# Attention with a running memory: the product with the probabilities made as columns, memory's part added after the transposes

## The reference, cut to what matters

```
sigma_q = elu(q) + 1;  sigma_k = elu(k) + 1
att_dot = softmax(mask(q k^T / scale)) @ v
att_mem = sigma_q @ mem / (sigma_q @ z)
delta   = v - sigma_k @ mem / (sigma_k @ z)
mem    += sigma_k^T @ delta;   z += sum(sigma_k)
att     = beta * att_mem + (1 - beta) * att_dot
out     = att.reshape(B, 64, 16*128) @ Wo
```

## Time and profile before

| | us |
|---|---|
| median of 3 runs | 1669.26 (1668.77 to 1669.92) |
| the profiled execution | 1669.3 |
| its span, first to last instruction | 1667.5 |
| PE busy | 1623.2 (97%) |
| DVE busy | 1143.7 (69%) |
| ACT busy | 884.9 (53%) |
| POOL busy | 497.9 (30%) |

### The profile page before, as it was taken

The page is one execution under the profiler, slowest core; times in us unless marked ns, Lnnn a source line. Parts: engine busy times, 40 slices in busy tenths (PEclk is TensorE's granted clock), DMA queues, the critical chain, the costliest instruction groups (busy, mean ns, idle before and its releaser), DMA issues.

```text
span 1667.5 us, 42642 instructions
## 1 busy us (share of the span) xinstructions
PE 1623.2 (97%) x17190; PEld 1418.9 (85%) x17190; DVE 1143.7 (69%) x3508; ACT 884.9 (53%) x1955; POOL 497.9 (30%) x438
## 2 busy tenths in 40 slices
PE   6899999999999999999999999999999999997998
PEld 5798999899998989998999989998999989875555
DVE  6865858586775757575776758585867757688544
ACT  5664646465563646364654646464655636451131
POOL 2332323232332313231333323232323323130351
PEclk9999999999999999999999999999999999998999
DMA  5102121212202121212112021212011021228847
GB/s 183 49 21 77 35 78 33 79 30 58 58 29 85 34 71 33 86 33 68 38 44 74 29 77 36 77 33 79 31 57 58 29 88 34 73 97 263 266 90 215
DMA packets 121780, 122.06 MB, mean 73 GB/s; under 512 B 24032, under 2 KB 101296, under 8 KB 121456
## 3 DMA queue, kind: packets, MB, share of 16 engines
q1 hardware_dynamic: 118224, 113.52, 22.3%
q0 software_dynamic: 3328, 5.81, 1.8%
q10 hardware_dynamic: 32, 0.01, 0.0%
HBM read 94.90 MB, written 24.40 MB: 72 GB/s over the span
## 4 chain that ended last, share of the span: by engine, by line
PE 93%; DVE 5%; issue 1%; ACT 1%; DMA 0%; DVEq 0%; ACTq 0%
PE bank_p L1473 23%; PE bank_v L1591 13%; PE chain_k L1546 6%; PE chain_k L1524 6%; PE bank_a L1481 5%; PE bank_v L1481 5%; PE chain_q L1524 5%; PE bank_s L1494 4%; PE chain L1524 3%; PE bank_a L1562 3%; PE bank_p L1504 3%; PE bank_p L1648 2%; PE bank_v L1573 2%; PE bank_a L1573 2%; PE bank_s L1579 2%; PE chain L1546 2%
## 5 line engine op out<-in xcount | busy, mean ns | idle before, releaser
L588 POOL TENSOR_TENSOR step_place<-step_place 128x512 f32<-128x512 f32 x128 | 166.7, 1303 | 575.5 <-ACT step_place L734 426.5
L756 ACT ACTIVATE step_place<-chain_q,step_place 128x128 f32<-128x128 f32 x384 | 113.3, 368 | 225.3 <-DVE step_place L990 225.3
L1591 PE MATMUL bank_v<-step_place 128*128 128x256 f32 x1024 | 225.3, 381 | 0.7 <-ACT step_place L767 0.7
L1473 PE MATMUL bank_p<-xt_hi,w_hi 128*128 128x256 f32 x1024 | 220.0, 296 | 4.6 <-DVE w_lo L911 2.5
L1591 PEld LDWEIGHTS bank_v<-step_place 128*128 128x128 f32 x1024 | 193.2, 190 | 29.2 <-issue 2.6
L1473 PE MATMUL bank_p<-xt_hi,w_lo 128*128 128x256 f32 x1024 | 206.6, 283 | 0.0
L1473 PE MATMUL bank_p<-xt_lo,w_hi 128*128 128x256 f32 x1024 | 206.4, 283 | 0.0
L625 POOL TENSOR_TENSOR step_place<-step_place 128x512 f32<-128x512 f32 x64 | 69.4, 1084 | 433.2 <-DVE step_place L1251 433.2
L1473 PEld LDWEIGHTS bank_p<-xt_hi,w_hi 128*128 128x128 f32 x1024 | 158.4, 191 | 24.0 <-issue 14.5
L978 DVE SCALAR_TENSOR_TENSOR step_place<-step_place,bank_p 128x512 f32<-128x512 f32 x128 | 87.5, 684 | 109.3 <-ACT bank_p L728 109.2
L1473 PEld LDWEIGHTS bank_p<-xt_hi,w_lo 128*128 128x128 f32 x1024 | 160.0, 192 | 0.0
(11 more groups left out here) (219 smaller groups left out, 3959.8 us busy)
## 6 DMA issues: line engine op xcount, KB each, us to landing
step_place<-in_L_attn_Wo_dram SPq DMA_DIRECT2D x128, 256.0 KB, 2.7
step_place<-beta_all SPq DMA_DIRECT2D x64, 256.0 KB, 3.4
expert_place<-in_L_ffn_w_dram SPq DMA_DIRECT2D x24, 512.0 KB, 7.6
expert_sums<-zero SPq DMA_DIRECT2D x16, 272.0 KB, 4.9
expert_rows<-rows_place SPq DMA_DIRECT2D x15, 288.0 KB, 2.3
step_place<-in_L_attn_x_dram SPq DMA_DIRECT2D x16, 256.0 KB, 3.9
turned<-in_L_attn_x_dram SPq DMA_DIRECT2D x16, 256.0 KB, 3.9
x_rows<-rows_place SPq DMA_DIRECT2D x16, 256.0 KB, 2.8
```

The lines of the kernel that those rows point to most:

```text
L588: nc.gpsimd.tensor_tensor(dl[seg][:, :, 0:DK], val[:, seg, :, :], beta_rows[:, :, :], ALU.mult).then_inc(s["vb_ready"], 1)
L756: ins = nc.scalar.activation(to[:, j, :], t[:, at:at + DK], ACT.Copy, scale=rd[:, seg, r:r + 1])
L1473: ins = mm(out, w[:, g, m, c, col], x[:, c, :, :].rearrange("p s t -> p (s t)"), start=i == 0, stop=i == len(parts) - 1)
L1591: ins = mm(bank_v[:, b * D:(b + 1) * D], att[:, b * PIECES + i, :], wo[:, i % WR, :], start=(i == 0 and b == 0), stop=(i == PIECES - 1), s ...
```

## The change

The product is made the other way round: `vo` (64 partitions x 128 columns) is the stationary operand and `pt` (64 x 64) the moving one, so that the result has the 128 value dimensions as rows and the queries as columns. It fills all 128 columns of the array and half its rows, as the matmuls of `update` do. Sequence 0 goes to `bank_a`, sequence 1 to `bank_v`. This result is already turned, so ACT copies it into `att` (now before `read_out` at the head of its step, each copy writing with a step of 128 elements between neighbours). The memory's read `am` alone goes through the transposes, and DVE adds the turned banks onto `att`; these additions now stand behind the first `sigma_k` of the step. One `by_piece` matrix suffices, since both segments of `am` now lie alike; the other is gone, with two instructions of GpSimd at the start.

```diff
@@ ScalarE: attended
-            for seg in range(2):
-                act.wait_ge(s["att_mm"], 2 * n + seg + 1)
-                rows = att[:, :, :].rearrange("p a (s g m) -> p a s g m", s=2, m=HG * QR)
+            act.wait_ge(s["av_mm"], n + 1)
+            for b in range(B):
+                rows = att[:, b * PIECES:(b + 1) * PIECES, :].rearrange(
+                    "p a (s g m) -> p s g m a", s=2, m=HG * QR)
                 nc.scalar.activation(
-                    rows[:, :, seg, g, :], seg_bank[seg][:, :].rearrange("p (a m) -> p a m", m=HG * QR),
-                    ACT.Copy).then_inc(s["att_ready"], 1)
+                    rows[:, :, g, :, :],
+                    seg_bank[b][:, :].rearrange("p (s m a) -> p s m a", s=2, m=HG * QR),
+                    ACT.Copy).then_inc(s["av_kept"], 1)
@@ ScalarE: body
+                if n:
+                    attended(n - 1, (g - 1) % NG, None if first or g == 0 else blk)
                 read_out(n, 0)
...
-                if n:
-                    attended(n - 1, (g - 1) % NG, None if first or g == 0 else blk)
@@ VectorE: attended
-            dve.wait_ge(s["av_mm"], n + 1)
             for seg in range(2):
-                dve.wait_ge(s["am_ready"], 2 * n + seg + 1)
-                t = (am[0][:, n % 2] if seg == 0 else am[1][:, 0]).rearrange("p j d -> p (j d)")
-                nc.vector.tensor_tensor(t, t, seg_bank[seg][:, :], ALU.add
-                                        ).then_inc(s["att_summed"], 1)
+                dve.wait_ge(s["att_mm"], 2 * n + seg + 1)
+                t = att[:, :, :].rearrange("p a (s g m) -> p a s g m", s=2, m=HG * QR
+                                           )[:, :, seg, n % NG, :]
+                nc.vector.tensor_tensor(
+                    t, t, seg_bank[seg][:, :].rearrange("p (a m) -> p a m", m=HG * QR), ALU.add
+                    ).then_inc(s["att_ready"], 1)
@@ VectorE: body
-                if n:
-                    attended(n - 1)
                 dve.wait_ge(s["s_mm"], n + 1)
...
                     sigma_k(n + 1, 0)
+                if n:
+                    attended(n - 1)
@@ TensorE: numerators
-                    half = b if seg == 0 or kind == 0 else 1 - b
-                    ins = mm(t[ROWS[half], at:at + ZC], sig[:, j, seg, b, :],
+                    ins = mm(t[ROWS[b], at:at + ZC], sig[:, j, seg, b, :],
@@ TensorE: attend
-                        half = b if seg == 0 else 1 - b
-                        ins = mm(seg_bank[seg][ROWS[half], j * DK:(j + 1) * DK],
-                                 pt[ROWS[b], j, seg, :], vo[ROWS[b], seg, j, :],
-                                 start=True, stop=True)
+                        c = (seg * HG + j) * SEG
+                        ins = mm(seg_bank[b][:, c:c + SEG], vo[ROWS[b], seg, j, :],
+                                 pt[ROWS[b], j, seg, :], start=True, stop=True)
@@ TensorE: attended_transposes
+            pe.wait_ge(s["av_kept"], 2 * n + 2)
             for seg in range(2):
-                pe.wait_ge(s["att_summed"], 2 * n + seg + 1)
+                pe.wait_ge(s["am_ready"], 2 * n + seg + 1)
...
-                    ins = nc.tensor.transpose(out[:, :, :, j, :], t[:, j, :], by_piece[seg][:, :])
+                    ins = nc.tensor.transpose(out[:, :, :, j, :], t[:, j, :], by_piece[:, :])
```

More of the change, by code:

```diff
@@ L43 @@
 KSCALE = 1.0 / (DK ** 0.5)
-STEP_PLACE = 24545
+STEP_PLACE = 24417
 def stand_alone(eng, noted):
@@ L205, in layer @@
     ident = sb("ident", [128, 128])
-    by_piece = [take([128, 128]) for i in range(2)]
+    by_piece = take([128, 128])
     turned = sb("turned", [128, NC * B * BLK])
@@ L274, in layer @@
              "s_masked s_max s_shifted s_exp s_inv p_ready pt_ready "
-             "rdk_ready rdq_ready mem3_ready wo_used x_turned dl_ready am_ready mem_ready att_summed att_ready "
+             "rdk_ready rdq_ready mem3_ready wo_used x_turned dl_ready am_ready mem_ready av_kept att_ready "
              "x1_ready x1_normed x1_stored x1t_mm x1t_ready x1t_stored lg_mm lg_exp "
@@ L555, in _ @@
         nc.gpsimd.memset(ident[:, :], 0.0).then_inc(s["ident_ready"], 1)
-        for i in range(2):
-            nc.gpsimd.memset(by_piece[i][:, :], 0.0).then_inc(s["ident_ready"], 1)
-        pool.wait_ge(s["ident_ready"], 3)
+        nc.gpsimd.memset(by_piece[:, :], 0.0).then_inc(s["ident_ready"], 1)
+        pool.wait_ge(s["ident_ready"], 2)
         nc.gpsimd.affine_select(out=ident[:, :], in_=ident[:, :], compare_op=ALU.not_equal,
@@ L561, in _ @@
                                 ).then_inc(s["ident_ready"], 1)
-        for i in range(2):
-            nc.gpsimd.affine_select(out=by_piece[i][:, :], in_=by_piece[i][:, :],
-                                    compare_op=ALU.not_equal, fill=1.0, base=-SEG * i,
-                                    pattern=[[-SEG + 2 * SEG * i, 2], [-1, PIECES], [-PIECES, QR]],
-                                    channel_multiplier=1).then_inc(s["ident_ready"], 1)
+        nc.gpsimd.affine_select(out=by_piece[:, :], in_=by_piece[:, :],
+                                compare_op=ALU.not_equal, fill=1.0, base=0,
+                                pattern=[[-SEG, 2], [-1, PIECES], [-PIECES, QR]],
+                                channel_multiplier=1).then_inc(s["ident_ready"], 1)
         nc.gpsimd.memset(mask[:, :], 0.0).then_inc(s["const_ready"], 1)
@@ L1616, in pick_transposes @@
                                 ident[:, :]).then_inc(s["pickt_mm"], 1)
-        pe.wait_ge(s["ident_ready"], 6)
+        pe.wait_ge(s["ident_ready"], 4)
         pe.wait_ge(s["x_normed"], 1)
```

## The result

The changed kernel takes 1747.72 us (median of 4 runs, 1746.33 to 1748.64) against 1669.01 of the kernel before, a ratio of 1.0471 with a 95% interval of 1.0455 to 1.0486: 79 us slower. The prediction said 1750 in a range of 1710 to 1768. Two of its executions, the traced one among them, took 1748.6 us at a mean granted clock of 0.989, the other two 1746.3 and 1746.9 at 0.993 and 0.992.

What follows compares the result with a forecast made beforehand. PE was taken to bound the kernel, busy for 97% of the span. 1669.3 us + 47 for PE's product + 34 for waits behind DVE's additions = 1750 us, range 1710 to 1768.

Steps and rivals of the forecast that it cites:

- PE's product: From `update` to `scores`: 16 matmuls with 128 stationary columns, 0.110 us apart, 0.74 us more a step, 47 us in all.
- The overflow of DVE: DVE's additions before `state_last` exceed its idle time, so PE's second half of the queries waits: 2.15 us a block, 34 in all.
- ACT hidden: ACT's two copies at the head of the step, some 0.6 us each, fit its 3.05 us idle before `read_out`: no cost.
- The bound, 1.5 us a copy: At the head of the step, ACT's copies cost time only beyond about 1.5 us for one copy.
- The rival built on DVE's accesses: Stepped access doubles DVE's additions to 1.19 us each: some 72 us on top, 1822 us; chance 0.06.
- PE waiting at the transposes for ACT: Sign that the prediction is wrong: ACT's copies should end before `read_out` is ready; no size given.
- the hidden overflow: Rival: loads set PE's pace in the product, but DVE's additions cause no visible wait: 1717 us; chance 0.18.
- the pace of the moving columns: Rival: moving columns set the product's distance at 0.062 us, with DVE's overflow still paid: 1701 us; chance 0.08.
- the upper bound: Top of the range, 1768 us: distance 0.113, additions 0.04 us longer, wait 0.15 us longer in each of 45 steps.

## Why the prediction was right

- PE's product: said 0.74 us a step from a distance of 0.110 us, measured 1.93 - 1.24 = 0.69, at 0.112. The small difference is mostly in the first distances behind `update`, which are 0.11 and 0.05 us; why the second is so short is not shown. In 64 steps it is 44 to 45 us in place of 47. The runs with half the columns and with four tiles show the cause, the loads.
- The overflow of DVE: said 0.57, 1.13, 0.45 and 0 us in g = 1, 2, 3 and 0, the 0.1 each for the loads that cannot run ahead included, 2.15 a block; measured 0.48, 0.99, 0.44 and 0, 1.91 a block. Sum 29 us by the run with the small works moved ahead, in place of 34: the 15 blocks were taken 3.6 us too high, and the last block costs 2.4 us where the prediction had some 4.
- ACT hidden: right in the steady steps, although the copies are 1.11 and 1.15 us and not 0.6. The bound, 1.5 us a copy, did the work. The Trainium skill's rule that an access which takes one element of each 16-byte line of SBUF pays (SBUF — State Buffer, "Door 1: The DMA port swizzle") agrees in direction: 1.11 us here against 0.60 for the same copy in runs of 16. No run tries a step between the two, so how much is due to the lines isn't shown. The rival built on DVE's accesses fell, because the additions write runs: 681 ns, as before. One of the prediction's own signs of being wrong, PE waiting at the transposes for ACT, came up once: for 2.0 us at the end of the loop.
- The end of the loop: missing. 6.5 us, of which 4.1 up to the routing's start through DVE's last list and 2.4 with the clock behind it. It made up for the terms that were 3 and 5 us too high: 44.5 + 29 + 6.5 = 80 against 79 measured. That the total is closer than its parts is luck.
- The rivals: the hidden overflow is out by the 47 waits, the pace of the moving columns by the run with 32 of them. Two sums of the prediction are a little off (1669.3 + 47 is 1716, and the terms of the upper bound add up to 1764, not 1768); the forecast doesn't rest on them.

## What to carry to other kernels

When a product is turned round to save a transpose, ask first what the new stationary side costs: with the moving side short, 128 stationary columns took 0.11 us with 32, 64 and 129 moving columns alike, and a form that keeps all tiles of the array in use (here 64x64, four side by side) beat one that halves the moving work (1.30 against 1.93 us for the same product). Before placing work into another engine's list, look for idle time at that very place in every variant of the step, since 1.2 us fitted in one of four and cost up to 1 us in the others; moving it elsewhere only helped where the new place had idle time of its own. And read the end of a loop separately: there the same edit met a different bound.

## What the runs showed of the hardware that I had not expected

- Four matmul records with their own loads of 64 columns each come every 0.058 us on four tiles, one record in 0.015 us; the number of instructions is not what bounds PE in this kernel.
- ACT's copy of 128x512 takes 1.11 to 1.15 us when it writes with a step of 512 bytes, 0.60 us when it writes runs of 16 elements.
- The granted clock fell to 0.50 (1.2 GHz) 0.5 us into PE's wait of 2.0 us for ACT at the end of the loop, 2.5 us after a wait of 1.3 us, and stayed there for 10.2 us; it stayed at 1.00 when PE had other products in that wait. The 3 us that it cost the product with `Wo` were covered by DVE's list.
- Behind the routing's start the granted clock fell once more in seven of the ten traces of the changed kernel and its variants, and the stretch to the end of the span was then 141.8 to 142.3 us in place of 138.8 to 140.0.
